# Depthwise weights expanded by DMA instead of by engines, and channels kept in their own order

## The reference, cut to what matters

```
x = x + L0(gn(x))   # focal modulation
x = x + L1(gn(x))   # deformable convolution
x = x + L2(gn(x))   # graph attention over 4096 nodes
x = x + L3(gn(x))   # 3x3 convolution of signs

L0(x):
  t = conv1x1(x)                    # 64 context channels and 4 gates
  ctx = t[:, :64]; all = 0
  for l, w in enumerate((fw3, fw5, fw7)):      # depthwise 3x3, 5x5, 7x7
      ctx = gelu(dwconv(ctx, w));  all += ctx * gate[l]
  all += mean(ctx) * gate[3]
  k = softmax(conv1x1(all, key_w)); qk = all @ k
  return all + conv1x1(relu(layernorm(conv1x1(qk, v1))), v2)

L1(x):
  value = conv1x1(x, vp); om = conv1x1(dwconv3x3(x, dw), om_w)
  ... bilinear gather of value by the offsets in om, weighted sum, conv1x1
```

## Time and profile before

| | us |
|---|---|
| median of three runs | 318.22 |
| lowest and highest | 316.47, 318.33 |
| the profiled execution | 316.38 |
| its span | 314.6 |

### The profile page before, as it was taken

How to read it: one execution, slowest core, us unless ns; L and a number is a source line. 1 busy time by engine, 2 the same in 40 slices (tenths; PEclk the granted TensorE clock), 3 DMA queues, 4 the chain that set the end, 5 groups by cost and what they waited for, 6 DMA issues and landing times.

```text
span 314.6 us, 6089 instructions
## 1 busy us (share of the span) xinstructions
PE 283.5 (90%) x2294; PEld 172.7 (55%) x2294; DVE 269.0 (85%) x404; ACT 168.3 (53%) x302; POOL 119.2 (38%) x163
## 2 busy tenths in 40 slices
PE   7788999589699999999999999569999999998995
PEld 7435997337354444567886644464433344357662
DVE  6789999798977599999988666984999999999763
ACT  1399563024250999940000003597889888999221
POOL 4003999983710669989997007000000000000000
PEclk9999999989999999999999999979999999999999
DMA  3421000000000000000000000353000000000003
GB/s 117 124 95 47 32 5 0 2 1 0 2 1 0 0 0 2 0 2 2 3 0 2 2 1 2 134 135 135 0 0 0 0 0 0 0 2 0 2 3 133
DMA packets 6462, 7.78 MB, mean 25 GB/s; under 512 B 2084, under 2 KB 4644, under 8 KB 6436
## 3 DMA queue, kind: packets, MB, share of 16 engines
q1 hardware_dynamic: 5684, 6.78, 6.9%
q10 hardware_dynamic: 752, 0.65, 0.7%
HBM read 4.28 MB, written 2.10 MB: 20 GB/s over the span
## 4 chain that ended last, share of the span: by engine, by line
PE 65%; DVE 13%; issue 10%; ACT 8%; ACTq 3%; DVEq 0%
PE ps L1483 15%; PE ps L1346 14%; PE ps L1360 9%; PE ps L1601 8%; PE ps L1497 6%; PE ps L1381 4%; ACT arena L886 3%; PE ps L1684 3%; ACT arena L869 2%; ACTq L393 2%; PE ps L1581 2%; ACT arena L667 1%; DVE arena L1261 1%; DVE arena L1244 1%; PE ps L1661 1%
## 5 line engine op out<-in xcount | busy, mean ns | idle before, releaser
L1601 PE MATMUL ps<-arena 128*128 (+1 forms) x256 | 63.3, 380 | 6.4 <-ACT arena L869 5.0
L869 ACT ACTIVATE arena<-ps 128x2048 f32<-128x2048 f32 x32 | 60.1, 1879 | 8.0 <-PE ps L1601 8.0
L1601 PEld LDWEIGHTS ps<-arena 128*128 (+1 forms) x256 | 24.3, 97 | 40.7 <-issue 14.1
L597 POOL TENSOR_TENSOR arena<-arena 128x768 f32<-128x768 f32 x21 | 40.2, 1950 | 4.8 <-ACT arena L772 4.6
L1244 DVE TENSOR_TENSOR arena<-arena 128x1024 f32 (+3 forms) x34 | 36.6, 1153 | 4.0 <-ACT arena L869 4.0
L1145 DVE TENSOR_TENSOR turns<-arena,ps 128x1024 f32<-128x1024 f32 x30 | 35.2, 1216 | 1.5 <-PE ps L1497 1.5
L1346 PE MATMUL ps<-turns,k 128*128 128x512 f32 x80 | 34.8, 593 | 0.1
L1483 PE MATMUL ps<-turns,shift 64*64 64x512 f32 x200 | 33.5, 592 | 0.0
L1360 PE MATMUL ps<-arena 64*64 64x240 f32 (+3 forms) x576 | 29.7, 361 | 4.2 <-issue 2.6
L1261 DVE TENSOR_TENSOR arena<-arena 128x1024 f32<-128x1024 f32 (+13 forms) x30 | 32.2, 1153 | 0.3
L1497 PE MATMUL ps<-arena,shift 64*64 64x256 f32 x192 | 30.6, 379 | 0.1
(11 more groups left out here) (239 smaller groups left out, 515.0 us busy)
## 6 DMA issues: line engine op xcount, KB each, us to landing
scratch_x<-xs SPq DMA_DIRECT2D x4, 256.0 KB
arena<-arena SPq DMA_DIRECT2D x2, 512.0 KB, 3.3
out<-arena SPq DMA_DIRECT2D x4, 256.0 KB, 2.1
xs<-in_x SPq DMA_DIRECT2D x8, 64.0 KB
xs<-in_x ACTq DMA_DIRECT2D x8, 64.0 KB
arena<-in_toep SPq DMA_DIRECT2D x1, 448.0 KB, 5.5
arena<-in_toep SPq DMA_DIRECT2D x1, 320.0 KB, 3.0
raw<-in_pw SPq DMA_DIRECT2D x8, 40.0 KB
```

Of the source, the lines that this page charges most:

```text
L597: pool.tensor_tensor(out=view(folds[i % len(folds)], dx * 3 * PX, [(PX, 3), (1, PX)]), in0=view(hy, (by - dy) * W + (dy * 3 + dx) * PX, [( ...
L869: act.activation(E[k], ps[:, (k % 2) * 2048:(k % 2 + 1) * 2048], ACT.Exp, scale=0.5 / SPLIT ** 2, accum_out=rowsum[:, bass.ds(i, 1)]).then ...
L1601: ins = pe.matmul(bank(b0 + q), w, m[:, bass.ds(i * P + 512 * q, 512)], start=(t == 0), stop=(t == 1 and q > 0))
```

## The change

- `wt3`, `wt7` and `wtd` are set to zero by GpSimd (`wt_zero`), and eight DMAs each write the bands straight into the diagonal blocks, with 16 partitions to a DMA. Nothing is spread on an engine. In a partition the order stays `[x][slot][row]`, so the 64 stationary columns of a matmul are read with a stride of 8k elements: 24 elements (96 bytes) for 3x3 and 56 elements (224 bytes) for 7x7 (`weights_in_place`).
- `wt5` is spread as before into adjacent columns, but in 16 instructions of 64 x 320: eight on ScalarE and eight on VectorE.
- The 3x3 and 7x7 take the channels in their own order and the 5x5 exchanges the two bits. `turn0` and `bias0` are gone. `key_v1` and `turned_x` bring small weights into the new order on GpSimd. A permutation `rows_back` (four copies on VectorE) takes the identity's place in the matmul that adds the context to the residual.
- The DMAs of `sX`, `keyb`, `rowN` and `v2raw` move from ScalarE's queue to SyncE's.

```diff
-        def bands(eng, dst, src, k, done):
+        def bands(eng, wt, src, k, done):
             w = 128 * k
-            eng.dma_start(dst, dram(src, 0, [(w, P), (1, w)])).then_inc(sem(done), 16)
+            for ch in range(8):
+                eng.dma_start(view(wt, (ch % 4) * w, [(1, w)], 16 * ch, 16), dram(src, ch * HW * w, [(w, HW), (1, w)])
+                              ).then_inc(sem(done), 16)
...
+        def weights_in_place(wt, k):
+            return lambda slot, row, i: view(wt, slot * k + row, [(8 * k, 64)], 64 * i, 64)
+        def weights_spread(wt, k):
+            return lambda slot, row, i: view(wt, (slot * k + row) * 64, [(1, 64)], 64 * i, 64)
...
         def _(sp):
             load_images(sp, (0, 1), 0)
             load_images(sp, (0, 1), 1)
-            bands(sp, band3, toep3, 3, "band3_in")
             load_images(sp, (0, 1), 2)
             load_images(sp, (0, 1), 3)
-            bands(sp, band7, toep7, 7, "band7_in")
+            sp.dma_start(band5, ...)
             sp.dma_start(sN, ...)
-            for p, row in swapped_rows:
-                sp.dma_start(view(bias0, ...))
-            bands(sp, band5, toep5, 5, "band5_in")
-            bands(sp, bandd, toepd, 3, "bandd_in")
+            sp.wait_ge(sem("wt_zero"), 1)
+            bands(sp, wt3, toep3, 3, "wt3_in")
+            sp.wait_ge(sem("wt_zero"), 2)
+            bands(sp, wt7, toep7, 7, "wt7_in")
+            sp.dma_start(sX, ...); keyb, rowN, v2raw
...
+            sp.wait_ge(sem("wt_zero"), 3)
+            bands(sp, wtd, toepd, 3, "wtd_in")
...
         def _(pool):        # inside the loop over mean256, pair_mean
+                for wt in ((wt3, wt7) if w == 16 else (wtd,)):
+                    pool.memset(wt, 0.0).then_inc(sem("wt_zero"), 1)
             pool.wait_ge(sem("fold_ready"), 3)
-            pool.wait_ge(sem("wt7_late"), 16 - WT7_ACT)
...
         def _(act):
-            act.dma_start(sX, ...); keyb, rowN, v2raw
             root(rstd[:, 0:2], view(mv, 1, [(2, 2)]))
-            act.wait_ge(sem("mask_ready"), 1)
-            act.wait_ge(sem("band7_in"), 16)
-            spread_wt7(3)
             root(rstd[:, 2:4], view(mv, 5, [(2, 2)]))
...
                 act.activation(o, ..., bias=sN[:, s:s + 1]).then_inc(sem("l0_pw_bias"), 1)
-                spread_wt7(1)
+                if i == 0:
+                    act.wait_ge(sem("band5_in"), 16)
+                spread_wt5((1, 1, 1, 2, 2, 1)[i])
...
         def _(dve):
             for h in range(2):
                 group_norm(xh, "xhat0", ..., 2 * h, 2)
-                spread_swapped(dve, wt3, band3, 3, "wt3_ready", swapped_parts[8 * h:8 * h + 8])
+            dve.wait_ge(sem("band5_in"), 16)
             for h in range(2):
+                for part in turned_parts[WT5_ACT + 4 * h:WT5_ACT + 4 * h + 4]:
+                    dve.tensor_scalar(...)            # 64 x 320 of wt5
                 dve.wait_ge(sem("l0_pw_bias"), 2 * h + 2)
                 for nq in (2 * h, 2 * h + 1):
                     dve.transpose(cols(tX, 0, PX, nq), to_rows_in(tN, nq)).then_inc(sem("t_turned"), 1)
-            spread(dve, wt5, band5, 5, "wt5_ready")
-            spread_swapped(dve, wt7, band7, 7, "wt7_late", swapped_parts[WT7_ACT:])
             dve.wait_ge(sem("l0_pw_bias"), 6)
...
         def _(pe):
-                    pe.wait_ge(sem(("wt3_ready", "wt5_ready", "wt7_ready")[l]), (16, 1, WT7_ACT)[l])
+                    pe.wait_ge(sem(("wt3_in", "wt5_ready", "wt7_in")[l]), (128, 16, 128)[l])
```

More of the change, by code:

```diff
@@ L112, in bass_preact_convs @@
         wt3, wt5, wt7, wtd = cut(0, 1536), cut(3072, 2560), cut(8192, 3584), cut(30976, 1536)
-        band3, band5, band7, bandd = cut(1536, 384), cut(1920, 640), cut(5632, 896), cut(32512, 384)
+        band5 = cut(1920, 640)
         mask4 = sb("mask4", 4)
-        turn0, bias0 = sb("turn0", 192), sb("bias0", 2)
-        rawv, biasd_in, biasd = sb("rawv", 128), sb("biasd_in", 16), sb("biasd", 8)
+        turned_x, key_v1 = sb("turned_x", 2 * SX_N), sb("key_v1", 40)
+        rows_back = sb("rows_back", P)
+        rawv, biasd = sb("rawv", 128), sb("biasd", 8)
         k0 = cut(34048, 768)
@@ L394, in load_images, with band5_part @@
                               dram(x, c4 * 512 + nq * 16384, [(2048, 8), (65536, 4), (1, 512)])).then_inc(sem(f"x_in{nq}"), 16)
-        def bands(eng, dst, src, k, done):
+        def bands(eng, wt, src, k, done):
             w = 128 * k
-            eng.dma_start(dst, dram(src, 0, [(w, P), (1, w)])).then_inc(sem(done), 16)
[L401 to L416, removed]
+            for ch in range(8):
+                eng.dma_start(view(wt, (ch % 4) * w, [(1, w)], 16 * ch, 16), dram(src, ch * HW * w, [(w, HW), (1, w)])
+                              ).then_inc(sem(done), 16)
+        turned_parts = [(gp, c4hi, b) for gp in range(2) for c4hi in range(2) for b in range(4)]
+        WT5_ACT = 8
+        def band5_part(gp, c4hi, b):
+            return (view(wt5, c4hi * 20 * 64 + 16 * b, [(1, HW), (64, 20)], 64 * gp, 64),
+                    view(band5, gp * 20, [(40, HW), (1, 20)], 64 * c4hi, 64), mask4[64 * c4hi:64 * c4hi + 64, b:b + 1])
         @block.sync
@@ L662, in _, with spread_wt5 @@
             spreads = [0]
[L664 to L669, removed]
+            def spread_wt5(n):
+                for part in turned_parts[spreads[0]:spreads[0] + n]:
+                    dst, src, mask = band5_part(*part)
+                    act.activation(dst, src, ACT.Copy, scale=mask).then_inc(sem("wt5_ready"), 1)
                 spreads[0] += n
             root(rstd[:, 0:2], view(mv, 1, [(2, 2)]))
-            act.wait_ge(sem("mask_ready"), 1)
-            act.wait_ge(sem("band7_in"), 16)
-            spread_wt7(3)
             root(rstd[:, 2:4], view(mv, 5, [(2, 2)]))
             act.wait_ge(sem("bias_in"), 16)
-            act.wait_ge(sem("bias0_in"), 128)
+            act.wait_ge(sem("mask_ready"), 1)
             for i, (h, s) in enumerate(pw_order):
@@ L1349, in pointwise, with depthwise @@
                 ins.then_inc(sem(ready), 1)
-            def depthwise(b0, wt, k, src, t, swapped, ready):
+            def depthwise(b0, weights, k, src, t, ready):
                 r = k // 2
@@ L1406, in _ @@
                     pe.wait_ge(sem("gelu"), need)
-                depthwise(2 * (m % CONV_PAIRS), (wt3, wt5, wt7)[l], (3, 5, 7)[l], (tX, ctxs[0], ctxs[1])[l], t, l != 1,
-                          "conv_done")
+                weights = (weights_in_place(wt3, 3), weights_spread(wt5, 5), weights_in_place(wt7, 7))[l]
+                depthwise(2 * (m % CONV_PAIRS), weights, (3, 5, 7)[l], (tX, ctxs[0], ctxs[1])[l], t, "conv_done")
                 if l == 2 and t > 1:
@@ L1427, in residual @@
             def residual(nq, src, first):
-                ins = pe.matmul(bank(4 + nq), ident, src[:, nq * 512:(nq + 1) * 512], start=first, stop=not first)
+                ins = pe.matmul(bank(4 + nq), ident if first else rows_back, src[:, nq * 512:(nq + 1) * 512],
+                                start=first, stop=not first)
                 if not first:
@@ L1440, in _ @@
             residual(3, xs, True)
+            pe.wait_ge(sem("rows_back"), 4)
             pe.wait_ge(sem("ctx_turned"), 1)
@@ L1470, in _ @@
                     pe.wait_ge(sem("value_bias"), 2)
-                depthwise(2 * t, wtd, 3, xX, t, False, "dw_done")
+                depthwise(2 * t, weights_in_place(wtd, 3), 3, xX, t, "dw_done")
             pe.wait_ge(sem("dw_bias"), 2)
```

103 lines of the change are left out of this document (48 added, 55 removed).

## The result

Ten runs of the changed kernel have a median of 315.96 us (314.61 to 318.34), ten of the kernel before 317.99 (316.33 to 318.35). The ratio is 0.9937, 95% interval 0.9913 to 0.9961: 2.0 us faster (1.2 to 2.8), less than one per cent. The profiled execution took 314.93 us with a span of 313.2, against 316.38 and 314.6: 1.4 us.

A forecast was written before the change was run, and what follows sets the result against it. TensorE was busiest, but VectorE was taken to end the first block. Front 2.6 and VectorE's lag 1.0 gave -3.6, + 0.3 (GpSimd) + 0 (strided loads) = -3.3 us: 313.1, or 314.0 from the runs' middle; range 311.3 to 318.6.

The forecast's parts named there:

- rival 2: Front not freed: images or `sN` land as before, or ScalarE's work is costlier; gain 1.5 to 2, about 315.6, chance 0.13.
- The front, by ScalarE's list: First block's start: ScalarE's biases and `wt5` parts set the convolutions' start, 26.1 instead of 28.76, gain 2.6 us.
- VectorE's old lag, 1.0 us: First block's end: VectorE, about 1.0 us behind TensorE, ends the block; that lag goes, 1.0 of the 3.6 us gain.
- the sign of a VectorE that is idle between the Gelus: First block's convolutions: VectorE idle between Gelus would show the forecast, its gate products starting 5.2 us earlier.
- Strided loads, 0: Convolutions' weight loads: 64 strided columns near 199 ns, rounds unchanged at 0.196 us; charge 0, bounds 0 and 2.5 us.
- Weights by DMA, 0: `wt3`, `wt7` and `wtd` zeroed by GpSimd and filled by DMA land in time, hidden by the pointwise stretch; cost zero.
- GpSimd in the tail, 0.3: GpSimd works next to VectorE's short tail and second norm; charge 0.3 us, bounds 0 and 1.2.

The follow-up runs named there:

- The undone move: Issues of sX, keyb, rowN and v2raw put back on ScalarE's queue in the changed kernel; ratio to the kernel before 0.9966 (0.9919 to 1.0012).
- The short filler in both kernels: 4 instead of 14 filler matmuls behind the convolutions; ratio to the kernel before 0.9965 in the kernel before, 0.9978 in the changed kernel.
- the series at 24: Matmuls with 32 moving columns and every 24th element as stationary columns, added to the changed kernel behind the convolutions; 0.127 us a round.

## Why the prediction was right, and where its terms were off

It forecast -3.3 us with 3.2 as the line between faster and the same; it came to -2.0. The direction and the mechanism of the front hold; two terms of the sum were mis-sized and one loss was missing. That the time lies in the range says little, since the range of 311.3 to 318.6 also holds the time before. The prediction gave 0.47 to a gain of more than one per cent and 0.39 to one within it, and the second came. The measured 315.96 is nearest to the 315.6 of rival 2 (chance 0.13), and one part of that rival was true: the images landed as before.

**The front, by ScalarE's list: right, 0.4 too large.** Forecast 26.1 for the convolutions, measured 26.54, gain 2.2 for 2.6. Inside it, the second piece of images was put at 7.5 and was awaited until 8.26, as before (8.21), though `band3` was gone; the last piece was put at 10 and was awaited until 11.89; and the scaling pair took 1.25 under a memset. TensorE started at 11.20 instead of 10.3, and the second square root, behind which the biases stand, ended at 13.19. So the list began 1.0 us late, with the first bias at 13.28 instead of 12.3. It then took 11.2 us instead of 11.8, with parts of 0.84 instead of 0.88 and waits for TensorE of 0.8 instead of 0.4: a bias and the part behind it overlap by about 0.1 us, which the prediction had not counted. This made good more than half of the delay. The undone move confirms the rule (root + 1.25, convolutions + 1.0). What the prediction did not see is why the list began late before: besides the four issues, `band7` with three parts, and the permuted bias.

**VectorE's old lag, 1.0 us: wrong.** The step failed where it said that the block ends by VectorE. VectorE did lag, but TensorE's filler and the keys behind it ended later still, and the filler moves with TensorE. The chain had said so: it runs through the filler, not through the sums. The timelines show the step behind the keys, before and then after, and in brackets how long VectorE stood for TensorE:

```profile
57.04 1.23 DVE L1008 TENSOR_TENSOR arena<-ps,arena 128x1024 f32<-128x1024 f32 x1 [1.48 <-PE ps L1416]
```
```profile
54.88 1.23 DVE L1003 TENSOR_TENSOR arena<-ps,arena 128x1024 f32<-128x1024 f32 x1 [0.82 <-PE ps L1410]
```

VectorE's last sum ends at 54.06, 1.5 us earlier than before. From the start of the convolutions to this step it takes 28.28 us before and 28.34 after, with or without VectorE's lag. The short filler in both kernels showed it: 1.4 us are free before, 0.8 after.

VectorE's lag did not go away either. Its last sum ends 3.3 us behind the last Gelu before (52.22 to 55.55) and 4.0 us behind it after (50.06 to 54.06), where the prediction had 2.35; VectorE was busy for 14.54 of the 15 us from 30 to 45, and the sign of a VectorE that is idle between the Gelus did not come. The groups of the gate products of the 5x5, before and then after, show where the time went:

```profile
L993 DVE TENSOR_TENSOR arena<-arena 64x256 f32<-64x256 f32 x16 | 6.9, 429 | 0.3
```
```profile
L988 DVE TENSOR_TENSOR arena<-arena 64x256 f32<-64x256 f32 x16 | 10.0, 626 | 0.9 <-ACT arena L695 0.6
```

The longest two took 1.15 and 1.18 us at 33.2 and 34.4, each next to one or two products of GpSimd of 1.2 and 1.5 us (lines 530 and 532). In the kernel before GpSimd made its like from 28.6 to 31.8, while VectorE transposed the gates. So both engines' products now meet in time. All kernels read with the new weights show means of about 500 to 640 ns here, the three with the old ones 429; that the meeting is the cause is argued from the traces, no run took GpSimd away.

**Strided loads, 0: right.** Forecast 199 ns, measured 195, rounds unchanged.

**Weights by DMA, 0: right.** The last band of `wt7` was issued by 15.83 us and takes 2.1 us to land by the median, and `wt7` was wanted at 31.6; the issues took 0.47 us instead of 0.69. GpSimd's list of block L1's weights, put at 33.5 to 80.5, began at 29.22 and ended near 72.8, so its cover was larger than the 2 us that the prediction counted. That GpSimd's memsets hold VectorE up was only charged in the tail; at the front they cost 4 us of VectorE's time, and next to nothing of the path, as the images came later still.

**GpSimd in the tail, 0.3: about right.** From the step behind the keys to the adding of the context the gain falls from 2.16 to 1.85 (71.12 instead of 72.97). The one loss found is the small step that took 0.35 before and 0.60 now, while GpSimd worked; that GpSimd is the cause is argued, not shown.

**A loss not forecast, 0.35.** At 204 us the graph block turns its operands. Windows of TensorE, before and then after, show the granted clock (fourth figure):

```profile
207.50:209.50 2.00, 2.00 (x27) 0.66 1.05 263
```
```profile
207.50:209.50 2.00, 2.00 (x36) 0.92 0.79 164
```

and the timelines, before and after, show the 64 transposes:

```profile
206.10 5.02 PE L1581 MATMUL ps<-ident,arena 128*128 128x128 f16 x64 [3.12 <-DVE arena L1214]
```
```profile
204.35 5.36 PE L1577 MATMUL ps<-ident,arena 128*128 128x128 f16 x64 [3.12 <-DVE arena L1210]
```

In both the clock falls to half for a stretch there. The work came 1.75 us earlier, but the stretch of half clock only 1.0 us (it ends at 207.8 instead of 208.9), so more of it lies on the transposes: 3.4 us instead of 2.75. If work at half clock takes twice its time, 0.65 us more of it costs 0.33, by estimate; the transposes take 5.36 instead of 5.02. The sum then reads 2.2 - 0.35 - 0.35 = 1.5, against 1.4 in the spans. This loss is read from two traces, no run made or removed it.

## What to carry to other kernels

A stationary operand of 64 float32 columns could be read here at steps of 96 and 224 bytes at the price of a step of 16, and where the moving operand is long enough that price is hidden: compare the pace of loads alone with the moving time of the shortest matmul. Before a lag of an engine is counted as gain, look for what else ends at that moment, filler included; the chain of waits shows only one of them. And ask of every constant-making GpSimd instruction what VectorE does under it: the memsets of `wt7` and `wtd` were nearly free under a wait for DMA, and started at 11.06, over the second pair of scalings, they came with the loss of the whole gain.

## What had not been expected of the hardware

Stationary loads of 64 columns in the four quadrants run side by side: 0.128 us a round for strided ones of about 210 ns each. The pace of the strided ones did not change when the granted clock fell from 1.00 to 0.50 in the middle of the series at 24. VectorE stood for 4 us under memsets that only write, and products of VectorE took up to 1.18 us instead of 0.42 next to products of GpSimd. With the clock granted by stretches of half speed, three runs of one kernel at a mean of 0.989 and two at 0.973 lie 3 us apart, more than the change brought.
